# Layer-3 products of a four-layer kernel in two parts of 256-column products, with the weight tiles' conversions placed elsewhere

## What is computed

```python
# layer 0: base weight + LoRA (8 adapters of rank 16, scaled), index in 1..7
x = x + (einsum('bsi,oi->bso', x, weight0) + bias0 + scale * (x @ A0[id].T @ B0[id].T))
# layer 1: base weight + LoRA (32 adapters of rank 16), index in 6..15
x = x + (einsum('bsd,od->bso', x, weight1) + bias1 + x @ A1[id].T @ B1[id].T)
# layer 2: a whole 1024 x 1024 matrix per batch, index in 3..7 (five in use)
x = x + einsum('bsi,boi->bso', x, W2[id])
# layer 3: a 64 x 64 matrix per batch, applied to the 64 rows of x, index in 0..15
x = x + einsum('bct,bcd->bdt', x, W3[id])
```

## Time and profile before

| | |
|---|---|
| median of three runs | 619.14 us |
| the profiled execution | 617.97 us |
| its span, first to last instruction | 616.2 us |
| mean granted TensorE clock | 0.991 of full |
| TensorE, matmul busy | 598.6 us, 97% of the span |
| TensorE, weight load busy | 496.5 us, 81% |
| VectorE busy | 304.2 us, 49% |
| ScalarE busy | 263.9 us, 43% |
| GpSimd busy | 56.6 us, 9% |
| share of the chain that ended last on PE | 79% |

### The profile page before, as it was taken

How to read it: one execution, slowest core, us unless ns; L and a number is a source line. 1 busy time by engine, 2 the same in 40 slices (tenths; PEclk the granted TensorE clock), 3 DMA queues, 4 the chain that set the end, 5 groups by cost and what they waited for, 6 DMA issues and landing times.

```text
span 616.2 us, 10822 instructions
## 1 busy us (share of the span) xinstructions
PE 598.6 (97%) x2870; PEld 496.5 (81%) x2871; DVE 304.2 (49%) x547; ACT 263.9 (43%) x337; POOL 56.6 (9%) x87
## 2 busy tenths in 40 slices
PE   8999999999989999999999899999999998999997
PEld 7888878888878887888888788888878874888885
DVE  6993220031686368453545845454584563535320
ACT  5632211033485184544527553552755372345111
POOL 3240001000012002000200200020021001000000
PEclk9999999999989999999999999999999997999999
DMA  8646723010054125423121642312164242021102
GB/s 312 236 170 68 86 87 139 18 52 17 2 207 158 53 48 194 172 70 98 41 68 36 204 172 70 98 41 68 36 204 172 70 155 84 17 87 36 36 1 69
DMA packets 66012, 60.92 MB, mean 99 GB/s; under 512 B 42050, under 2 KB 50242, under 8 KB 65988
## 3 DMA queue, kind: packets, MB, share of 16 engines
q1 hardware_dynamic: 65988, 60.63, 33.1%
HBM read 49.33 MB, written 11.27 MB: 98 GB/s over the span
## 4 chain that ended last, share of the span: by engine, by line
PE 79%; issue 6%; DVE 5%; ACT 4%; DMA 2%; ACTq 1%; DVEq 1%; POOL 1%; SPq 0%; POOLq 0%
PE y_ps L1064 22%; PE y_ps L1101 22%; PE y_ps L1018 11%; PE t_ps L1018 5%; PE t_ps L1092 5%; DVE ring L859 2%; PE y_ps L999 2%; PE low_ps L1056 2%; DMA arena<-wt 2%; ACTq L224 1%; PE y_ps L995 1%; PE t_ps L999 1%; PE low_ps L999 1%; ACT ring L547 1%; DVE arena L864 1%
## 5 line engine op out<-in xcount | busy, mean ns | idle before, releaser
L1101 PE MATMUL y_ps<-ring,ops 128*128 128x512 f32 (+1 forms) x792 | 190.3, 396 | 7.1 <-DVE ring L859 4.2
L1101 PEld LDWEIGHTS y_ps<-ring,ops 128*128 128x128 f32 (+1 forms) x792 | 145.8, 186 | 44.4 <-issue 7.9
L1064 PE MATMUL y_ps<-wm,ops 128*128 128x512 f32 x768 | 180.5, 393 | 0.0
L1064 PEld LDWEIGHTS y_ps<-wm,ops 128*128 128x128 f32 x768 | 142.7, 189 | 29.3 <-DVE arena L864 0.2
L1018 PE MATMUL y_ps<-ring,wm 128*128 128x512 f32 x240 | 55.3, 390 | 0.0
L859 DVE TENSOR_TENSOR ring<-arena,ring 128x1024 fp32r<-128x1024 f32 x40 | 48.9, 1271 | 12.2 <-ACT ring L547 12.0
L1018 PEld LDWEIGHTS y_ps<-ring,wm 128*128 128x128 f32 x240 | 44.9, 188 | 9.3
L520 ACT CAST ops<-arena 128x512 fp32r<-128x512 f32 x32 | 19.4, 620 | 70.3 <-PE y_ps L1064 70.3
L547 ACT CAST ring<-arena 128x1024 fp32r<-128x1024 f32 x40 | 40.4, 1049 | 15.9 <-POOL arena L431 15.8
L1092 PEld LDWEIGHTS t_ps<-w_split,ops 128*128 128x128 f32 x384 | 45.9, 194 | 1.2
L431 POOL TENSOR_TENSOR arena<-arena,ident 128x128 f32<-128x128 f32 x40 | 24.5, 622 | 236.6 <-DMA arena<-wt 233.3
(11 more groups left out here) (142 smaller groups left out, 565.6 us busy)
## 6 DMA issues: line engine op xcount, KB each, us to landing
arena<-wt SPq DMA_DIRECT2D x48, 512.0 KB, 4.6
arena<-xt SPq DMA_DIRECT2D x32, 256.0 KB, 2.8
out<-arena SPq DMA_DIRECT2D x30, 256.0 KB, 3.1
arena<-w SPq DMA_DIRECT2D x8, 576.0 KB, 5.3
a_stage<-a_tab SPq DMA_DIRECT2D x64, 64.0 KB, 1.9
arena<-b_tab SPq DMA_DIRECT2D x64, 64.0 KB, 2.0
arena<-a_cols SPq DMA_DIRECT2D x8, 256.0 KB, 4.1
a_tab<-bias SPq DMA_DIRECT2D x4, 256.0 KB, 8.5
```

The lines of the kernel that those rows point to most:

```text
L1064: op = nc.tensor.matmul(y_ps[:, cols], xs[:, k, part_x, :], wm[:, k, part_w, cols], start=k == 0 and part_x == part_w, stop=False)
L1101: op = nc.tensor.matmul(y[0:m, cols], xs2[:, k, part_x, 0:m], ring[:, k, part_w, cols], start=k == 0 and part_x == part_w, stop=k == KT - ...
```

## The change

Layer 3 of a pair takes 16 products of 256 columns instead of 24 of 128: the high and the low part of `w3_split` stand side by side as one moving operand of 256 columns, so that one product with x2's high (or low) part gives both. This computes lo·lo too. The part multiplied by w3's high part and the part multiplied by its low part lie beside each other in `t_ps`, which is therefore full (1024 columns) after half of the tiles. So there are two parts, (j, 0) and (j, 1), of 8 products each. Part 0 stands between the halves of layer 2, part 1 ahead of the last tile of the second half (`between(1)` at k == KT - 1). Each part is evicted by four operations in place of two: ACT copies the w3-high part into `xs2` (as fp32r) and the w3-low part into x2's buffer (fp32), DVE subtracts the first from the second and then adds the full w3-high part from PSUM. Part 1 on PE waits for the eviction of part 0 (`xs2_lo_ready`), and `take_x2` waits for the last eviction of the pair before.

In the loop, the order on ACT and DVE changes too. The four further copies of the B tables (`b_again_parts`) stand behind `xs2_hi(j, 0)` and ahead of tiles 0 to 3; `couple(j)` moves into step j, behind the first `split_low`; of tiles 4 to 7 only tile 4 stays ahead of the second LoRA chain (now `finish_low`), and tiles 5 to 7 stand behind `split_w3`, ahead of `x_hi` and `take_x2`. The SP and POOL programs are unchanged.

```diff
+        def t_of(part):
+            return t_ps[:, :].rearrange("p (k s r) -> p k s r", s=2, r=P)[:, :, part]
+        def t_lo_of(h):
+            return x2[:, BANKS[h]].rearrange("p (k r) -> p k r", r=P)
...
             def xs2_hi(j, h):
-                act.wait_ge(t_done, j + 1)
+                act.wait_ge(t_done, 2 * j + (h + 1))
                 if not (isinstance(j, int) and j == 0):
                     act.wait_ge((half_used, l2_done)[h], j)
-                nc.scalar.copy(xs2_of(h, 0), t_of(h)).then_inc(xs2_hi_ready, 1)
+                nc.scalar.copy(xs2_of(h, 0), t_of(0)).then_inc(xs2_hi_ready, 1)
+                nc.scalar.copy(t_lo_of(h), t_of(1)).then_inc(t_lo_ready, 1)
...
@@ ScalarE @@
+            def step(j, last=False):
+                take_out(j - 2)
+                xs2_hi(j - 1, 1)
+                second_half_of_next(j - 2, SECOND_HALF[:1])
                 if not last:
                     a_hi(j + 1)
                 split_w3(j)
+                second_half_of_next(j - 2, SECOND_HALF[1:])
                 if not last:
+                    for h in range(2):
+                        x_hi(j + 1, h)
                 x2_hi(j)
                 if not last:
                     b_hi_parts(j + 1)
+                behind_layer2(j - 1)
                 xs2_hi(j, 0)
+                if not last:
+                    for layer in range(2):
+                        b_again_parts(layer)
+                first_half_of_next(j - 1)
...
             def take_x2(j):
                 dve.wait_ge(y_done, j + 1)
+                if not (isinstance(j, int) and j == 0):
+                    dve.wait_ge(xs2_lo_ready, 2 * j)
...
             def xs2_lo(j, h):
-                dve.wait_ge(xs2_hi_ready, 2 * j + (h + 1))
-                nc.vector.tensor_tensor(xs2_of(h, 1), t_of(h), xs2_of(h, 0), ALU.subtract).then_inc(xs2_lo_ready, 1)
+                at = 2 * j + (h + 1)
+                dve.wait_ge(t_lo_ready, at)
+                nc.vector.tensor_tensor(t_lo_of(h), t_lo_of(h), xs2_of(h, 0), ALU.subtract).then_inc(t_lo_left, 1)
+                dve.wait_ge(t_lo_left, at)
+                nc.vector.tensor_tensor(xs2_of(h, 1), t_of(0), t_lo_of(h), ALU.add).then_inc(xs2_lo_ready, 1)
...
@@ VectorE @@
+            def step(j, last=False):
+                sum_low(j, 0)
+                split_low(j, 0)
+                couple(j)
+                sum_low(j, 1)
+                xs2_lo(j - 1, 1)
+                second_half_of_next(j - 2, SECOND_HALF[:1])
+                finish_low(j)
                 if not last:
                     a_lo(j + 1)
                 split_w3(j)
+                second_half_of_next(j - 2, SECOND_HALF[1:])
                 if not last:
+                    for h in range(2):
+                        x_lo(j + 1, h)
                 take_x2(j)
                 x2_lo(j)
                 if not last:
                     b_lo_parts(j + 1)
+                behind_layer2(j - 1)
                 xs2_lo(j, 0)
+                first_half_of_next(j - 1)
...
-            def transposes(j):
+            def transposes(j, h):
+                if h == 0:
+                    pe.wait_ge(x2_lo_ready, j + 1)
+                    pe.wait_ge(w3_lo_ready, j + 1)
+                if not (isinstance(j, int) and j == 0 and h == 0):
+                    pe.wait_ge(xs2_lo_ready, 2 * j + h)
+                for k in range(HK):
+                    cols = slice((h * HK + k) * P, (h * HK + k + 1) * P)
+                    to = t_ps[:, 2 * k * P:2 * (k + 1) * P]
+                    for part_x in range(2):
+                        op = nc.tensor.matmul(to, x2_split[:, part_x, cols], w3_split[:, :, :].rearrange("p s r -> p (s r)"),
+                                              start=part_x == 0, stop=part_x == 1)
                 op.then_inc(t_done, 1)
```

More of the change, by code:

```diff
@@ L583, in second_half_of_next @@
                     act.wait_ge(l2_done, j + 1)
[L584 to L593, removed]
+                    convert(rank + mixed + 1, tiles)
@@ L608, in step @@
                     b_hi_parts(j + 1)
[L609 to L614, removed]
+                behind_layer2(j - 1)
                 xs2_hi(j, 0)
-                with act.If(following != 0):
-                    act.wait_ge(half_used, j)
-                    convert(rank + mixed + 1, FIRST_HALF)
+                if not last:
+                    for layer in range(2):
+                        b_again_parts(layer)
+                first_half_of_next(j - 1)
             for i in range(3):
@@ new lines, in behind_layer2, with first_half_of_next, first_step @@
+            def behind_layer2(j):
+                rank, mixed = first_rank(dve, j), mixed_of(dve, j)
+                with dve.If(mixed != 0):
+                    convert(rank + 1, range(KT))
+            def first_half_of_next(j):
+                rank, mixed, following = first_rank(dve, j), mixed_of(dve, j), following_of(dve, j)
+                with dve.If(following != 0):
+                    convert(rank + mixed + 1, FIRST_HALF)
+            def first_step():
+                sum_low(0, 0)
+                split_low(0, 0)
+                sum_low(0, 1)
+                convert(0, (0, 1))
+                finish_low(0)
+                a_lo(1)
+                split_w3(0)
+                x_lo(1, 0)
+                convert(0, (2, 3))
+                x_lo(1, 1)
+                take_x2(0)
+                sum_low(1, 0)
+                split_low(1, 0)
+                b_lo_parts(1)
+                couple(1)
+                sum_low(1, 1)
+                x2_lo(0)
@@ new lines, in second_step @@
+            def second_step():
+                convert(0, (4, 5))
+                finish_low(1)
+                a_lo(2)
+                convert(0, (6, 7))
+                xs2_lo(0, 0)
+                for h in range(2):
+                    x_lo(2, h)
+                xs2_lo(0, 1)
+                split_w3(1)
+                take_x2(1)
+                x2_lo(1)
+                b_lo_parts(2)
+                behind_layer2(0)
+                xs2_lo(1, 0)
+                first_half_of_next(0)
@@ L943, in _ @@
             dve.wait_ge(plan_ready, 1)
[L944 to L945 removed]
+            first_step()
+            second_step()
             with dve.Fori(2, PAIRS - 1) as j:
[L947 to L948 removed]
+                step(j)
+            step(PAIRS - 1, last=True)
             j = PAIRS
             xs2_lo(j - 1, 1)
[L952 to L955 removed]
+            second_half_of_next(j - 2, SECOND_HALF)
+            behind_layer2(j - 1)
         @block.tensor
```

160 lines of the change are left out of this document (68 added, 92 removed).

## The result

Four runs of the changed kernel gave 622.85 to 625.98 us, median 624.21, against 618.88 for the kernel before: a ratio of 1.0088, 95% interval 1.0059 to 1.0118. It is slower, as forecast, by half of what was forecast (5.3 us against 10.4). The profiled execution took 622.85 us, with a span of 621.0, 4.8 more than before. The sum forecast for such an execution was 628.5 us of device time.

A forecast was written before the change was run, and what follows sets the result against it. It took what PE executes as the bound. Three places +18.5, mixed pair -2.0, first two pairs -1.0 and other seven -5.0 gave +10.5 us: 628.5 by the profile, 629.5 by the median, range 620 to 636.

The forecast's parts named there:

- Products: Layer 3 of each pair: 16 products at 0.12 us replace 24 at 0.110, saving 0.71 us a pair.
- Steps 1 and 2: Where a matrix follows: B copies delay tile 0 by 2.3 us; SP's queue shifts as a whole, a_hi at 352.9.
- Step 3: Where a matrix follows: first LoRA chain released at 345.5, PE there at 344.7; new wait of 0.9 us at between_loras.
- Steps 4 and 5: Tiles 5 to 7 ahead of take_x2: transposes at 364.0, PE waits 6.4 us, step ends 4.2 us later.
- Step 6: The clock falls after the 6.4 us wait where a matrix follows, costing 2.6 us, between 1.7 and 3.5.
- The three places together: Three places where a matrix follows: +6.1 us each, the first maybe 0.3 worse; together +18.5 us.
- The mixed pair: Tiles no longer behind B copies; about 3.3 of 4.2 us of waits stay; -2.0 us (-3.5 to +0.5).
- The first two pairs: The 1.6 us wait at L1071 goes, part (0, 1) waits for eviction; net -1.0 us (-3 to +2).
- Rival A: Pile-up at the three places does not decide, only savings count: 600.0 us by profile, 601 by median; chance 0.10.
- B: Queue shift partly absorbed, or 3 us wait with clock held; each place costs 0 to 3: 612 to 620; chance 0.08.
- C: New wait in every pair, part 0's eviction missing its 1.0 us slack: 642 us; chance 0.08.
- D: Layer 3 products cost more than LoRA's, 0.227 each: +1 us a pair; chance 0.02.

The follow-up runs named there:

- the B copies' experiment: Changed kernel with the four B copies put back ahead of xs2's first half on ScalarE; 641.73 us, 1.0369 of the kernel before.
- spare products: Changed kernel with 20 spare 512-column products into a free PSUM bank ahead of layer 3's part 0 at the three places; 620.73 us.
- tiles 4 to 7 together: Changed kernel with all of tiles 4 to 7 ahead of the second LoRA and A tables on both engines; 620.04 us.
- B copies behind tiles: Changed kernel with the four B copies moved behind tiles 0 to 3, tiles 5 to 7 left in place; 620.83 us.
- both edits: Changed kernel with B copies behind tiles 0 to 3 and tiles 4 to 7 together ahead of the second LoRA chain; 615.56 us.
- finish first: Changed kernel, B copies behind tiles 0 to 3, VectorE finishing second LoRA before tiles 4 to 7 in one block, ScalarE's ahead of A tables; 610.48 us.
- half of x behind x2: Finish first kernel with the second half of the next pair's x converted behind x2 on ScalarE and VectorE; 611.07 us.
- the store later: Half of x behind x2 kernel with SP's store moved behind the loads of the mixed pair's tiles 4 to 7; 608.71 us.

## Why the prediction came out so

It was right in sign, in the place and in the cause: tiles 5 to 7 behind the A tables hold up x2, and moving them alone makes the kernel before slower. Its +10.5 us of span were +4.8. By its own steps:

*Products*: 0.71 a pair forecast, 0.79 measured (0.119 a product against 0.12). Right. The Trainium skill's figures ("TensorE: Matmul & The Clock Gate", Back-to-back issue gap: about 81 ns for 128 columns and 131 for 512), by which the saving would have been half of that, don't hold here: 109 and 227 ns.

*What bounds the kernel*: rows 1 name three lines, not four, and leave out 2.5 us of waits in the setup and the first pairs. Nothing rests on it.

*Eviction*: no wait in ordinary pairs. Right, and its margin shown by the B copies' experiment.

*Steps 1 and 2 (tile 0 later by 2.3 us, and SP, and the A tables with it)*: from part 0 to tile 0 it is 6.82 us instead of 4.48, 2.3 more; to a_hi 22.1 us instead of 19.7, 2.4 more. Right.

*Step 3 (a new wait of 0.9 at between_loras)*: 0.47 there.

*Steps 4 and 5 (364.0, a wait of 6.4)*: part 0 to part 0 33.72 us (333.60 to 367.32), forecast 33.1. So x2 was even 0.6 us later than I said, but PE did not wait 6.4 at one line: 4.9 there, 0.8 at the second LoRA and 0.8 of issue behind it, which I had let go. The step was wrong in one thing, the time at which DVE begins tile 4: there are 1.7 us without work ahead of it, so the second LoRA's finish is late as before.

*Step 6 (the clock)*: 2.6 forecast, 1.7 to 1.9 measured, at the lower end of its bounds; the spare products show that it is the clock.

*The three places together*: the three intervals are 20.8 us longer, and the ones ahead of them 3.1 shorter, together +17.7; forecast +18.5. Right. (The 3.1 are three savings of 0.79 and a gap of 0.8 us ahead of T1, with nothing that PE could be seen to wait for, which is gone.)

*The mixed pair*: forecast -2.0, measured -5.4 (45.01 to 39.57), outside its bounds (-3.5 to +0.5). This is the term that was mis-sized, 3.4 of the 5.7 us by which the sum missed. Of the 5.4 us 0.8 are products and 1.6 waits: one wait of 2.6 is left instead of two of 4.2 in all. The other 3.0 us are the clock, which fell in the kernel before and not here; the products for the 64 rows left (128*64 in the row) ran at full pace:

```profile
504.98 1.24 SPq L349 DMA_DIRECT2D out<-arena  x2
508.42 11.15 PE L1172 MATMUL y_ps<-ring,ops 128*128 128x512 f32 x48
508.96 4.63 DVE L887 TENSOR_TENSOR ring<-arena,ring 128x1024 fp32r<-128x1024 f32 x4
510.37 3.72 SPq L278 DMA_DIRECT2D arena<-wt  x4
522.17 4.35 PE L1172 MATMUL y_ps<-ring,ops 128*64 128x512 f32 x18 [2.60 <-DVE ring L887]
```

That the clock held looks like luck of this execution: in all eight other kernels with the change's 256-column products it fell there, behind waits as short as 2.53 us (in the one with products of 128 columns it held). The table has seven of them (T3's wait is PE's largest there; the lag is from DVE's end of tile 0 to SP's issue of tile 4 in the mixed pair; times in us, read from the timelines):

| kernel | wait in T3 | SP's lag, mixed | wait in mixed | 18 products behind it |
|---|---|---|---|---|
| after | 4.95 | 0.2 | 2.60 | 4.35 |
| tiles 4 to 7 together | 4.45 | 0.2 | 2.80 | 5.92 |
| B copies behind tiles | 4.59 | 0.2 | 2.53 | 5.93 |
| spare products | none, filled | 0.2 | 3.66 | 5.92 |
| both edits | 2.98 | 1.6 | 4.37 | 5.95 |
| finish first | 2.52 | 3.4 | 6.08 | 5.78 |
| half of x behind x2 | 1.91 | 2.8 | 5.20 | 5.92 |
| the store later | 2.70 | 0.2 | 2.65 | 5.93 |

The table shows a second thing that the prediction lacks: T3 and the mixed pair behind it are not apart. Where PE waits 4.4 us or more at T3, SP has its store out in time (504.98 above) and sends tile 4 off as soon as its stage is free (510.37). Where PE waits 3 us or less, SP is still busy with the store, tile 4 goes out 1.6 to 3.4 us late, and PE's wait in the mixed pair grows by about as much, unless the store is moved. In the finish-first kernel PE waits 4.5 us less at T3 than in the changed kernel, its waits at the two LoRAs included, and 3.5 of them came back in the mixed pair. The spare products are not a case of this: their lag is 0.2, and why the wait there is 1.1 us longer stays open.

*The first two pairs*: -1.7 against -1.0, and setup -0.2. This agreement is luck. The products save 1.6 and the waits cost 1.6 more (2.2 and 0.8 of issue, where it was 1.6, each a little longer by the starts); the rest, 1.9 us, is the clock, which fell in the second pair of the kernel before and not in that of the changed one (stretch, us, PE busy, granted clock, DMA share, GB/s). Before, behind the wait of 1.6 us; after, behind the wait of 2.2; and the kernel with both edits, where it fell too and the two pairs take 0.3 us longer than before:

```profile
183.00:184.00 1.00, 1.00 (x3) 0.50 0.23 66
```

```profile
190.00:195.00 5.00, 5.00 (x25) 1.00 0.03 7
```

```profile
190.00:195.00 5.00, 5.00 (x16) 0.64 0.02 3
```

*The other seven pairs*: -5.5 against -5.0. Right.

So 4.9 us of the difference between the two profiled executions (3.0 and 1.9) are the clock's, in two stretches for which the forecast had no such term. Had it fallen there in both, the sum would be +9.7, an estimate from these rows, next to the +10.5 forecast. The profiled execution is the fastest of four; the others have spans 1.3 to 3.2 us longer at a granted clock of 0.980 to 0.985 instead of 0.988. So the clock fell more in them, and where it did is open. In the median, too, the result is half of the forecast, and how much of that is the clock's is not shown.

Rival A asked for a_hi by 346.5 and was rightly put low; B's 612 to 620 lies just under the result, but its mechanism, places of 0 to 3 us, isn't there; C and D fell. What I missed among the rivals is that VectorE's queue alone, without the A tables, costs 3 us at such a place.

## What to carry to other kernels

Work that stands behind a wait in an engine's program becomes as late as that wait, even if it was ready long before: here three tile conversions behind a table load cost about 19 us on the kernel before. In the changed kernel two moves together took off 13.7 us (624.21 to 610.48), which is 1.3% under the kernel before: the B copies behind tiles 0 to 3, and on VectorE first the short chain that another engine needs and then the long block without a break. A saving on the busiest engine only counts in stretches where the others have slack; list the few irregular stretches, and price neighbours together, since a wait in one lets the queues catch up for the next. After a change to such an order, compare the distance from pair to pair, not the totals, and in it the waits apart from the pace of the products: a clock that fell in one execution and held in the other is worth 2 to 3 us in one stretch, as much as a move.

## What the runs showed of the hardware

- A matmul with a new weight load and 128 columns takes 0.109 us, with 256 columns 0.119, with 512 0.227.
- Ahead of the conditional block with tile 4 VectorE stands 1.5 to 1.9 us without work in the kernels looked at (1.72 in the row at 352.14, 1.73 at 348.28), although what it converts is ready, and ScalarE 0.97 ahead of tiles 5 to 7 (357.58). I take it for the block's own control, which a split into two blocks would pay twice; no run takes the condition out, so this is not shown.
- Waits of 2 to 3 us do not always bring the clock down. Behind 2.53 us it held (finish-first, T2), behind 2.98 it fell (both edits, T2: 24 products in 8.35 us). In one execution (half of x behind x2) it held behind 1.89 at T2 and fell behind 1.91 at T3. In the mixed pair it held behind 2.60 (after) and fell behind 2.53 (B copies behind tiles). At equal code, executions differ by this: the changed kernel's runs lie between 622.85 us at a mean granted clock of 0.988 and 625.98 at 0.980.
- 20 useless products in each of three waits of 5 us kept the clock up (mean granted 0.996 instead of 0.988) and made each place 1.7 to 2.1 us shorter.
